# The expert results' gathers of columns 0 to 11: waits on counted tiles, and their sums on GpSimd

## The chip, the cores and the metric

One Trainium2 chip, one of its cores. The metric is the device time of one execution in microseconds (us); a measurement is the median of several executions.

## What is computed

The input x has 2 x 1024 rows of 256 numbers. Each row is layer-normed to xn, and the output is x plus two branches of xn, cut here to what matters:

```python
# attention branch: tokens of 16 numbers, windows of 8, two half-heads with a 3-tap convolution,
# a projection, a layer norm over 16, a residual; written back transposed
# expert branch: 2048 rows, 16 experts, 6 chosen for each row
scores = sigmoid(xn @ gate_weight.T)
topk_idx, topk_weight = gate(scores, bias)      # 2 of 4 groups, then 6 of their 8 experts
for e in range(16):
    inter = silu(xn @ gate_proj[e].T) * (xn @ up_proj[e].T)
    out += comb[:, e:e+1] * (inter @ down_proj[e].T)
out += shared expert of 352 hidden units on every row
return x + attention(xn) + out
```

## The kernel before, in words

The 2048 rows lie in SBUF as 128 lanes by 16 *columns* of 256 numbers; `yacc` holds x in this layout and collects every term of the output. A first stage (to about 104 us) normalises the rows, computes the routing on VectorE (`routing`, L1211) and runs the shared expert. Each chosen pair of row and expert gets a *slot*, a row number in a DRAM table `xs_dram`; `slot_i` holds, for each lane, column c and choice k (0 to 5), the slot at place c * 8 + k, sorted by falling slot. GpSimd scatters the rows to their slots with 96 indirect DMAs (L594), 16 columns by 6 choices.

The experts then run over 111 *tiles* of 128 slots (constant NT; loops over t on all engines, TensorE's at L1055, VectorE's at L1649). Tile t is loaded by SyncE from `xs_dram` (L491), transposed (L981, copied by ScalarE L725), multiplied by the gate and up weights (L991), made to `inter_s` by ScalarE's silu (L733) and VectorE's product (L1532), transposed again (L1007, L740), multiplied by the down weights (L1014), copied to one of four buffers `y_s` (ScalarE L753, in four tiles VectorE L1556) and stored by SyncE to `y_dram` (L496). The semaphore `y_sb` counts these copies, `put[i]` the stores of buffer i that have landed. Three pieces of other work are threaded by hand through the tile loop: the attention of four blocks on VectorE (`attention`, steps per tile by `attention_quota`), whose last step ends about tile 80; transposes and projections on TensorE (tiles 87 to 98); and `normalise` (L1570), one VectorE step per tile from tile 100 on, in which L1598 adds the attention branch to four columns of `yacc` at a time.

Slots are dealt so that early columns come early: an expert's rows are in column order, and the tiles of all experts are dealt in parts that end with columns 5, 9, 12, 14, 15, 16 (`MARKS`). `DONE` gives, for each first column, how many tiles must be stored at most before its results are complete, whatever the routing: 69 for columns 0 to 8, 87 for 9 to 11, 99 for 12 and 13, 105 for 14, 111 for 15.

The results come back by 42 *fetches* (`FETCHES`): seven groups of columns (0-2, 3-5, 6-8, 9-11, 12-13, 14, 15) by six choices. A fetch is one indirect DMA (L614) for each of its columns, into one of seven places (`places`, 768 numbers wide); that makes 72 DMAs for columns 0 to 11 and 24 for the rest. GpSimd issues them in order; before a group it waits for the stores of `DONE` tiles (`stored`, L599), and before a place is filled again it waits that the sum of the fetch before it is done (L607). VectorE adds each fetch to `yacc` (`add_results`, L1605, one instruction at L1614): fetches 0 to 23 at fixed tiles from tile 76 on (`ADD_AT`), the rest among the last steps of `normalise` and behind them. Last, SyncE and ScalarE store the columns (`store_out`, L444).

Of the kernel before, what the change touches and what calls it, by code (L numbers as in the profile page):

```python
# [126 lines left out]
ADD_AT = {}  # L127
for _n in range(24):
    ADD_AT.setdefault(76 + 14 * _n // 9, []).append(_n)


def place_of(n):

    return n % FEW if n < 2 * FEW else n % PLACES
# [61 lines left out]
def build(nc, x, wall, wexp, consts, out):  # L196
    ctx = ExitStack()
    with ctx:
# [16 lines left out]
        y_dram = nc.dram_tensor("y_dram", [NT * P, H], F32).ap()  # L215
# [20 lines left out]
        pad_row = at("pad_row", [1, NE], I32)  # L236
        blk_at = cursor[0]
# [59 lines left out]
        whole = at("whole", [P, (len(MARKS) + 1) * NE], I32)  # L297
        assert cursor[0] <= after_w, cursor[0] - after_w
# [17 lines left out]
        added = sem("added")  # L316
# [140 lines left out]
        def _(sp):  # L457
# [20 lines left out]
            sp.wait_ge(weights_ok, 1)  # L478
            sp.wait_ge(m_ok, UNITS)
# [42 lines left out]
        def _(pool):  # L522
# [80 lines left out]

            for n, (first, last, k) in enumerate(FETCHES):
                if k == 0 and first in DONE:
                    stored(first)
                if before_at(n) is not None:  # L607

                    pool.wait_ge(added, before_at(n) + 1)
                elif n >= FEW:  # L610
                    pool.wait_ge(att_ok, 2 * B)
                for c in range(first, last):
                    o, there = c * KEEP + k, (c - first) * H
                    nc.gpsimd.indirect_dma_start(places[place_of(n)][:, there:there + H], None,  # L614
                                                 y_dram[0:DONE[max(d for d in DONE if d <= first)] * P, :],
                                                 bass.IndirectOffsetOnAxis(slot_i[:, o:o + 1], 0)).then_inc(got[place_of(n)], 16)

# [197 lines left out]
        def _(pe):  # L815
# [41 lines left out]
            def qkv_job(n):  # L857
# [42 lines left out]
            def expert_rows():  # L900
# [3 lines left out]
                                 skip_group_check=True).then_inc(erow_ps, 1)  # L904

# [60 lines left out]
            for s in range(UNITS):  # L966
# [113 lines left out]
        def _(dve):  # L1080
# [130 lines left out]
            def routing():  # L1211
# [154 lines left out]

                one = work[:, 0:1]
# [13 lines left out]
            def tile_experts():  # L1381
# [5 lines left out]
                nc.vector.tensor_scalar(e_row[:, :], misc[0][0:1, 384:384 + RT], float(H), None, ALU.add).then_inc(rows_ok, 1)  # L1387

# [181 lines left out]
            def normalise():  # L1570
# [17 lines left out]
                for b in range(NBLK):  # L1588
# [7 lines left out]
                    settle()  # L1596
                    dve.wait_ge(added, sums.value())
# [21 lines left out]
            for u in range(-1, UNITS):  # L1619
# [29 lines left out]
            for t in range(NT):  # L1649
# [17 lines left out]
                for n in ADD_AT.get(t, ()):  # L1667
                    add_results(n)
# [57 lines left out]
```

## Time and profile before

| | |
|---|---|
| median of 3 runs (lowest to highest) | 457.14 us (451.7 to 457.64) |
| the profiled execution's own time | 456.78 us |
| its span in the profile | 455.0 us |
| TensorE busy | 400.8 us (88%) |
| VectorE busy | 364.8 us (80%) |
| ScalarE busy | 224.8 us (49%) |
| GpSimd busy | 234.7 us (52%) |
| 96 scatters, GpSimd L594 | 111.4 us, 1160 ns each |
| VectorE add of 768 columns, L1614 | 950 ns |

Busy shares are averages over stages. GpSimd's 52% is made of three stretches with long waits between them, and TensorE's 88% ends at 425 us, thirty before the span does. So a stage is read by its own timeline: which engine works without a gap there, and what the others wait for. The start of an instruction is taken from the timeline, and the time that it takes from its queue is the distance to the next start (its spacing), which can be shorter than its duration where the engine overlaps two.

### The profile page before, as it was taken

How to read it: one execution, taken by the hardware profiler on the slowest of the kernel's cores; microseconds unless marked ns; L12 is line 12 of the kernel's file. 1: busy time of each engine (PE TensorE's matmuls, PEld its weight loads, DVE VectorE, ACT ScalarE, POOL GpSimd, SP SyncE). 2: the span in 40 equal slices, each digit the busy share in tenths (PEclk: the TensorE clock that was granted, in tenths of full speed). 3: DMA queues.
4: the chain of work that ended last, by engine and by line, in shares of the span. 5: the costliest groups of instructions: out<-in, count | busy, mean ns of one | idle time of the engine just before them, and what ended most of it. 6: DMA issues, size and time to landing. Idle time of an engine off the chain costs nothing.

```text
span 455.0 us, 7300 instructions
## 1 busy us (share of the span) xinstructions
PE 400.8 (88%) x1989; PEld 310.2 (68%) x1989; DVE 364.8 (80%) x593; ACT 224.8 (49%) x616; POOL 234.7 (52%) x221
## 2 busy tenths in 40 slices
PE   7799599999999999997999999989989999999200
PEld 7688499889767677675777777767667777767200
DVE  2869953686899989999799999999995355479951
ACT  3654234325564445653476864675437744554200
POOL 3530156775777777873000000007787777778671
PEclk9889979999999999999899999999999999999755
DMA  7998422226455766576733334336657997665652
GB/s 169 330 412 354 163 107 88 98 76 223 132 184 190 205 207 197 184 229 184 216 114 103 97 95 121 103 90 169 196 166 202 287 234 194 175 198 160 201 151 81
DMA packets 55878, 80.55 MB, mean 177 GB/s; under 512 B 8480, under 2 KB 47264, under 8 KB 55584
## 3 DMA queue, kind: packets, MB, share of 16 engines
q1 hardware_dynamic: 42912, 50.91, 36.7%
q0 software_dynamic: 9216, 25.96, 18.8%
q10 hardware_dynamic: 3712, 3.21, 2.4%
q8 instruction: 19, 0.31, 0.3%
q14 instruction: 19, 0.16, 0.1%
HBM read 43.48 MB, written 36.57 MB: 176 GB/s over the span
## 4 chain that ended last, share of the span: by engine, by line
PE 49%; DVE 22%; issue 12%; DMA 5%; POOL 4%; ACT 2%; SPq 2%; ACTq 1%; DVEq 1%; POOLq 0%
PE gate L991 15%; PE ps_y L1014 10%; POOL xs_dram L594 4%; PE ps_y L942 4%; DVE prod L1094 4%; DVE qkv L1094 4%; PE up L920 3%; PE ps_y L1007 3%; DVE inter_s L1532 3%; PE up L981 3%; DVE sc L1094 2%; PE gate L920 2%; DVE yacc L1614 2%; PE misc L882 2%; PE misc L1041 2%
## 5 line engine op out<-in xcount | busy, mean ns | idle before, releaser
L991 PE MATMUL gate<-wrec,xgT 128*128 x444 | 151.3, 463 | 2.9 <-ACT xgT L725 1.8
L594 POOL DMA_INDIRECT xs_dram<-xrow,slot_i x96 | 111.4, 1160 | 50.6 <-DMA xs_dram<-xrow,slot_i 21.5
L1014 PE MATMUL ps_y<-wrec,interT 88*128 x444 | 115.2, 382 | 0.0
L614 POOL DMA_INDIRECT gat<-y_dram,slot_i x50 | 55.0, 1099 | 113.6 <-DMA y_dram<-y_s 98.9
L991 PEld LDWEIGHTS gate<-wrec,xgT 128*128 128x128 f32 x444 | 75.8, 190 | 28.2 <-issue 4.4
L1014 PEld LDWEIGHTS ps_y<-wrec,interT 88*128 88x128 f32 x444 | 76.0, 191 | 6.7 <-issue 0.3
L1532 DVE SCALAR_TENSOR_TENSOR inter_s<-gate,xg,gate_s 128x176 f32<-128x176 f32 x111 | 43.6, 393 | 33.8 <-ACT gate_s L733 32.9
L733 ACT ACTIVATE gate_s<-gate 128x176 f32<-128x176 f32 x111 | 35.2, 317 | 70.1 <-PE ps_y L1007 67.7
L753 ACT ACTIVATE y_s<-ps_y 128x256 f32<-128x256 f32 x107 | 41.0, 383 | 55.7 <-PE up L981 52.6
L1007 PEld LDWEIGHTS ps_y<-ident,inter_s 128*88 128x88 f32 x222 | 26.7, 123 | 37.6 <-issue 19.3
L1007 PE MATMUL ps_y<-ident,inter_s 128*88 128x128 f32 x222 | 42.7, 274 | 5.0 <-DVE y_s L1556 2.8
L981 PE MATMUL up<-ident,xg 128*128 128x128 f32 x222 | 42.8, 274 | 3.7 <-DMA xg<-xs_dram 3.7
L981 PEld LDWEIGHTS up<-ident,xg 128*128 128x128 f32 x222 | 31.4, 143 | 15.7 <-DMA xg<-xs_dram 4.5
L725 ACT ACTIVATE xgT<-up 128x256 f32<-128x256 f32 x107 | 40.4, 379 | 0.2 <-PE up L981 0.2
L740 ACT ACTIVATE interT<-ps_y 88x256 f32<-88x256 f32 x107 | 39.9, 373 | 1.1 <-PE ps_y L1007 1.1
L1094 DVE TENSOR_TENSOR prod<-sc,qkv 128x1024 f32<-128x1024 f32 x32 | 38.4, 1215 | 0.1
L1094 DVE TENSOR_TENSOR sc<-sc,prod 128x1024 f32<-128x1024 f32 x28 | 34.1, 1219 | 0.2
L1094 DVE TENSOR_TENSOR prod<-qkv 128x1024 f32<-128x1024 f32 x28 | 33.6, 1216 | 0.0
L1094 DVE TENSOR_TENSOR qkv<-qkv,prod 128x1024 f32<-128x1024 f32 (+1 forms) x28 | 33.0, 1179 | 0.1
L652 ACT ACTIVATE qkv<-misc 128x192 f32<-128x192 f32 x40 | 14.9, 438 | 27.4 <-PE misc L882 18.8
L614 POOL DMA_INDIRECT prod<-y_dram,slot_i x20 | 20.8, 1039 | 6.1 <-issue 5.2
L614 POOL DMA_INDIRECT spare<-y_dram,slot_i x16 | 19.8, 1240 | 5.9 <-issue 3.7
(215 smaller groups left out, 633.8 us busy)
## 6 DMA issues: line engine op xcount, KB each, us to landing
xg<-xs_dram SPq DMA_DIRECT2D x111, 136.0 KB, 2.6
y_dram<-y_s SPq DMA_DIRECT2D x111, 128.0 KB, 2.1
wrec<-wexp SPq DMA_DIRECT2D x14, 608.0 KB, 15.1
xs_dram<-zrow SPq DMA_DIRECT2D x1, 2176.0 KB, 13.0
xn_dram<-xrow SPq DMA_DIRECT2D x8, 256.0 KB
qkv<-xn_dram SPq DMA_DIRECT2D x8, 256.0 KB
xs_dram<-xrow,slot_i POOLq DMA_INDIRECT x96, 2.9
wrec<-wexp SPq DMA_DIRECT2D x1, 1216.0 KB, 5.6
```

The lines of the kernel that those rows point to most:

```text
L594: nc.gpsimd.indirect_dma_start(xs_dram[0:DONE[max(d for d in DONE if d <= c)] * P, :], bass.IndirectOffsetOnAxis(slot_i[:, o:o + 1], 0), x ...
L614: nc.gpsimd.indirect_dma_start(places[place_of(n)][:, there:there + H], None, y_dram[0:DONE[max(d for d in DONE if d <= first)] * P, :], b ...
L725: nc.scalar.activation(xgT[:, t % 2, :], guB[t % 2][:, 0:H], ACT.Copy).then_inc(xt_sb, 1)
L733: nc.scalar.activation(gate_s[:, t % 2, :], guA[t % 2][:, 0:I], ACT.Silu).then_inc(gate_ok, 1)
L740: nc.scalar.activation(interT[:, t % 2, :], ps_y[0:HALF, t % 2 * 2 * H + H:(t % 2 + 1) * 2 * H], ACT.Copy).then_inc(it_sb, 1)
L753: nc.scalar.activation(y_s[:, t % YRING, :], ps_y[:, t % 2 * 2 * H:t % 2 * 2 * H + H], ACT.Copy).then_inc(y_sb, 1)
L981: last = nc.tensor.transpose(guB[t % 2][:, k * P:(k + 1) * P], xg[:, t % RING, k * P:(k + 1) * P], ident[:, :])
L991: last = nc.tensor.matmul(guA[t % 2][:, 0:2 * I], xgT[:, t % 2, k * P:(k + 1) * P], wrec[:, bass.ds(record + k * 2 * I, 2 * I)], start=(k ...
L1007: last = nc.tensor.transpose(ps_y[0:HALF, o:o + P], inter_s[:, t % 2, k * HALF:(k + 1) * HALF], ident[:, :])
L1014: last = nc.tensor.matmul(ps_y[:, t % 2 * 2 * H:t % 2 * 2 * H + H], interT[:, t % 2, k * P:(k + 1) * P], wrec[0:HALF, bass.ds(record + KT ...
L1094: do(nc.vector.tensor_tensor(o, a, b, op))
L1532: nc.vector.scalar_tensor_tensor(inter_s[:, t % 2, :], guA[t % 2][:, I:2 * I], xg[:, t % RING, bass.ds(weight, 1)], gate_s[:, t % 2, :], A ...
```

## The change

For each of the first four groups of three columns (fetches 0 to 23, `OWN`) the kernel now counts the tiles that really have to be done. The highest slot of each lane and column (`tops`) is transposed and reduced to the highest slot of each group, and `tiles_done` turns it into a tile count plus 4 in `done_row`. GpSimd loads these four numbers into registers and waits for `y_sb` to reach them, where it waited for the stores of 69 or 87 tiles: a copy into a `y_s` buffer waits for the store of four tiles before, so the count plus 4 says that the stores have landed. A tiny multiply (L634 of the changed kernel) stands behind the wait.

The sums of fetches 0 to 23 move from VectorE to GpSimd: behind the DMAs of fetch n, it adds fetch n-1 (`own_sum`). These 24 fetches use four places in turn. `ADD_AT` is gone; VectorE keeps fetches 24 to 41. The results are stored into the first 256 numbers of the rows of `xs_dram`, in place of `y_dram`, so GpSimd multiplies `slot_i` by the row's 272 numbers first. In the changed kernel TensorE's second projection job behind the shared expert (L909 there) and SyncE's load of the last two experts' weights (L489 there) also wait for `done_ok`.

```diff
+COUNTED = 4
+OWN = COUNTED * TOP
+TOPS_AT, COUNTS_AT = 8, 10
...
-    return n % FEW if n < 2 * FEW else n % PLACES
+    return n % FEW if n < OWN else n % PLACES
...
-            engine.wait_ge(added, TOP * sum(first < c1 for first, _ in GROUPS))
+            engine.wait_ge(pool_added, min(OWN, TOP * sum(first < c1 for first, _ in GROUPS)))
...
+            sp.wait_ge(done_ok, 1)
             sp.wait_ge(m_ok, UNITS)
...
-                sp.dma_start(y_dram[t * P:(t + 1) * P, :], y_s[:, t % YRING, :]).then_inc(put[t % YRING], 16)
+                sp.dma_start(xs_dram[t * P:(t + 1) * P, 0:H], y_s[:, t % YRING, :]).then_inc(put[t % YRING], 16)
...
+            def own_sum(n):
+
+                first, last, _ = FETCHES[n]
+                acc = yacc[:, first * H:last * H]
+                pool.wait_ge(got[place_of(n)], 16 * fetched(n))
+                if n:
+                    pool.wait_ge(pool_added, n)
+                nc.gpsimd.tensor_tensor(acc, acc, places[place_of(n)][:, 0:(last - first) * H], ALU.add).then_inc(pool_added, 1)
+
+            landed(pool, sent, TOK * TOP)
+            nc.gpsimd.tensor_scalar(slot_i[:, :], slot_i[:, :], float(XW), None, ALU.mult).then_inc(rows_at, 1)
+            pool.wait_ge(rows_at, 1)
+            pool.wait_ge(y_ok, NBLK)
+            pool.wait_ge(done_ok, 1)
+            counted = [nc.gpsimd.value_load(done_row[0:1, g:g + 1], min_val=YRING + 1, max_val=NT) for g in range(COUNTED)]
             for n, (first, last, k) in enumerate(FETCHES):
-                if k == 0 and first in DONE:
+                if k == 0 and n < OWN:
+
+                    pool.wait_ge(y_sb, counted[n // TOP])
+                    nc.gpsimd.tensor_tensor(expo[:, 0:1], expo[:, 1:2], expo[:, 2:3], ALU.mult)
+                elif k == 0 and first in DONE:
                     stored(first)
...
+                if 1 <= n < OWN:
+                    own_sum(n - 1)
+                if n == OWN - 1:
+                    own_sum(n)
...
                 if n == EARLY_JOBS + 1:
 
                     pe.wait_ge(rows_ok, 2)
+                    pe.wait_ge(done_ok, 1)
...
+            def tiles_done():
+
+
+                dve.wait_ge(last_ps, 1)
+                groups = last_f[0:1, 0:COUNTED]
+                do(nc.vector.tensor_reduce(groups, misc[0][0:1, P:P + COUNTED * WIDE].rearrange("p (g c) -> p g c", c=WIDE), AX.X, ALU.max))
+                settle()
+                do(nc.vector.tensor_scalar(last_i[:, :], groups, P - 1.0, None, ALU.add))
+                settle()
+                do(nc.vector.tensor_scalar(last_i[:, :], last_i[:, :], 7, None, ALU.logical_shift_right))
+                settle()
+                nc.vector.tensor_scalar(done_row[:, :], last_i[:, :], float(YRING), None, ALU.add).then_inc(done_ok, 1)
...
+                    dve.wait_ge(pool_added, min(OWN, TOP * sum(first < (b + 1) * TILES for first, _ in GROUPS)))
                     dve.wait_ge(added, sums.value())
...
             y_sum(NBLK - 1)
+            tiles_done()
...
-                for n in ADD_AT.get(t, ()):
-                    add_results(n)
```

The order of GpSimd's instructions at the first fetches, before: the 96 scatters end, and the fetches follow each other with nothing between.

```order
L594 DMA xs_dram<-xrow,slot_i 14208x272 x6
L614 DMA gat<-y_dram,slot_i 128x256 x9
L614 DMA spare<-y_dram,slot_i 128x256 x3
L614 DMA gat<-y_dram,slot_i 128x256 x9
L614 DMA spare<-y_dram,slot_i 128x256 x3
```

The same place on GpSimd in the changed kernel (L605 is the scatter, L647 the fetch's DMA, L622 the sum).

```order
L605 DMA xs_dram<-xrow,slot_i 14208x272 x6
L625 TENSOR_SCALAR slot_i<-slot_i 128x128
...
L634 TENSOR_TENSOR expo<-expo 128x1
L647 DMA gat<-xs_dram,slot_i 128x256 x6
L622 TENSOR_TENSOR yacc<-yacc,gat 128x768
L647 DMA gat<-xs_dram,slot_i 128x256 x3
L622 TENSOR_TENSOR yacc<-yacc,gat 128x768
L647 DMA spare<-xs_dram,slot_i 128x256 x3
L622 TENSOR_TENSOR yacc<-yacc,gat 128x768
```

A sum of 128 x 768 now stands in the one queue behind every three DMAs, 24 in all.

VectorE's order in tiles 75 to 77, before: two steps of attention between the products L1532, and from here on a sum L1614 in most tiles.

```order
L1532 SCALAR_TENSOR_TENSOR inter_s<-gate,xg,gate_s 128x176
L1522 TENSOR_TENSOR qkv<-qkv,prod 128x1024
L1094 TENSOR_TENSOR prod<-sc,qkv 128x1024
L1614 TENSOR_TENSOR yacc<-yacc,gat 128x768
L1532 ISA
L1532 SCALAR_TENSOR_TENSOR inter_s<-gate,xg,gate_s 128x176
L1094 TENSOR_TENSOR prod<-sc,qkv 128x1024
L1094 TENSOR_TENSOR qkv<-qkv,prod 128x1024
L1614 TENSOR_TENSOR yacc<-yacc,gat 128x768
```

The same place on VectorE in the changed kernel (L1606 is the product, L1596 and L1148 are attention).

```order
L1606 SCALAR_TENSOR_TENSOR inter_s<-gate,xg,gate_s 128x176
L1596 TENSOR_TENSOR qkv<-qkv,prod 128x1024
L1148 TENSOR_TENSOR prod<-sc,qkv 128x1024
L1606 ISA
L1606 SCALAR_TENSOR_TENSOR inter_s<-gate,xg,gate_s 128x176
L1148 TENSOR_TENSOR prod<-sc,qkv 128x1024
L1148 TENSOR_TENSOR qkv<-qkv,prod 128x1024
```

The sums are gone from there, and the attention steps stand in the same tiles as before.

VectorE's order at the end of the changed kernel, behind the last product L1606 (L1673 is the add of the attention branch, L1148 its two steps, L1689 `add_results`).

```order
L1606 SCALAR_TENSOR_TENSOR inter_s<-gate,xg,gate_s 128x176
L1148 TENSOR_TENSOR qkv<-qkv,prod 128x256x4
L1148 TENSOR_TENSOR qkv<-qkv 128x256x4
L1673 TENSOR_TENSOR yacc<-yacc,qkv 128x1024
L1689 TENSOR_TENSOR yacc<-yacc,spare 128x512
L1148 TENSOR_TENSOR qkv<-qkv,prod 128x256x4
L1148 TENSOR_TENSOR qkv<-qkv 128x256x4
L1689 TENSOR_TENSOR yacc<-yacc,sc 128x512
L1673 TENSOR_TENSOR yacc<-yacc,qkv 128x1024
L1689 TENSOR_TENSOR yacc<-yacc,prod 128x512 x2
```

The first sum that VectorE does is that of fetch 24 (into the place `spare`), behind the third L1673.

## Rows read from the trace of the kernel before

**Rows 1.** The page: the span, and GpSimd's busy tenths in 40 slices.
```profile
span 455.0 us, 7300 instructions
POOL 3530156775777777873000000007787777778671
```

**Rows 2.** L614: what GpSimd sat idle for before it (us, times), and time to landing.
```profile
  DMA y_dram<-y_s: 98.9, 2
DMA to landing us min/median/max: 2.7/3.4/6.4
```

**Rows 3.** Timeline of GpSimd: start us, us, engine, line, operation; fetches' DMAs 1, 25, 73, 91, 96.
```profile
308.58 1.93 POOL L614 DMA_INDIRECT gat<-y_dram,slot_i  x1 [97.89 <-DMA y_dram<-y_s]
...
345.30 1.41 POOL L614 DMA_INDIRECT gat<-y_dram,slot_i  x1 [0.30 <-issue]
...
409.29 1.04 POOL L614 DMA_INDIRECT spare<-y_dram,slot_i  x1 [0.30 <-issue]
...
437.81 1.08 POOL L614 DMA_INDIRECT gat<-y_dram,slot_i  x1 [0.30 <-issue]
...
445.45 0.95 POOL L614 DMA_INDIRECT prod<-y_dram,slot_i  x1 [0.30 <-DVE yacc L1614]
```

**Rows 4.** Timeline of ScalarE and VectorE: two copies into y_s.
```profile
281.80 0.38 ACT L753 ACTIVATE y_s<-ps_y 128x256 f32<-128x256 f32 x1 [0.50 <-PE up L981]
...
306.14 0.41 DVE L1556 COPY y_s<-ps_y 128x256 f32<-128x256 f32 x1
```

**Rows 5.** Stretches: us; busy (count) of PE, PEld, DVE, ACT, POOL; PEclk, DMA share, GB/s.
```profile
282.00:345.00 63.00, 59.56 (x282) 43.09 (x281) 61.04 (x79) 35.47 (x102) 29.40 (x24) 1.00 0.51 147
345.00:409.00 64.00, 62.94 (x326) 46.74 (x325) 35.08 (x65) 37.05 (x108) 49.37 (x48) 1.00 0.80 217
```

**Rows 6.** Timeline of GpSimd: arithmetic on two inputs in SBUF, and a cast.
```profile
19.43 1.82 POOL L548 TENSOR_TENSOR w_lo<-raw,w_hi 128x768 fp32r<-128x768 f32 x1
21.20 0.89 POOL L554 CAST w_hi<-raw 128x768 fp32r<-128x768 f32 x1
...
44.52 1.29 POOL L559 TENSOR_TENSOR in_lo<-sil,in_hi 128x512 fp32r<-128x512 f32 x1 [17.77 <-ACT in_hi L674]
```

**Rows 7.** Timeline of VectorE in the same stretches.
```profile
18.65 0.40 DVE L1122 TENSOR_SCALAR xrow<-yacc,rstd,mv 128x256 f32<-128x256 f32 x1
...
19.57 1.83 DVE L1122 TENSOR_SCALAR xrow<-yacc,rstd,mv 128x256 f32<-128x256 f32 x1
21.33 0.68 DVE L1113 TENSOR_TENSOR xT_lo<-misc,xT_hi 128x512 fp32r<-128x512 f32 x1
...
45.04 0.90 DVE L1094 TENSOR_TENSOR sc<-sc 128x112 f32<-128x112 f32 x1
...
46.40 0.87 DVE L1094 TENSOR_TENSOR sc<-sc 128x112 f32<-128x112 f32 x3
```

**Rows 8.** Timeline of VectorE: the last attention step, and a sum.
```profile
338.40 1.23 DVE L1524 TENSOR_TENSOR qkv<-qkv,prod 128x1024 f32<-128x1024 f32 x1
339.54 0.95 DVE L1614 TENSOR_TENSOR yacc<-yacc,gat 128x768 f32<-128x768 f32 x1
340.41 0.40 DVE L1532 SCALAR_TENSOR_TENSOR inter_s<-gate,xg,gate_s 128x176 f32<-128x176 f32 x1
```

**Rows 9.** Timeline of VectorE at the end.
```profile
420.48 0.40 DVE L1532 SCALAR_TENSOR_TENSOR inter_s<-gate,xg,gate_s 128x176 f32<-128x176 f32 x1
...
430.34 1.88 DVE L1598 TENSOR_TENSOR yacc<-yacc,qkv 128x1024 f32<-128x1024 f32 x1
...
448.25 0.43 DVE L1614 TENSOR_TENSOR yacc<-yacc,prod 128x256 f32<-128x256 f32 x1 [0.46 <-DMA prod<-y_dram,slot_i]
```

**Rows 10.** Timeline of VectorE and TensorE behind the shared expert.
```profile
104.35 1.66 DVE L1407 SCALAR_TENSOR_TENSOR yacc<-ps_y,cst,yacc 128x256 f32<-128x256 f32 x4 [0.66 <-PE ps_y L942]
...
106.07 0.55 PE L882 MATMUL ps_y<-blk_hi,xT_hi 128*128 128x384 f32 x1 [0.35 <-DVE yacc L1407]
```

**Rows 11.** The chain that ended last, before tile 39 starts: start us, us, what.
```profile
209.55 2.63 DMA xs_dram<-xrow,slot_i
```

More of the change, by code:

```diff
@@ L236, in build @@
         pad_row = at("pad_row", [1, NE], I32)
+        done_row = at("done_row", [1, COUNTED], I32)
         blk_at = cursor[0]
@@ L297, in build @@
         whole = at("whole", [P, (len(MARKS) + 1) * NE], I32)
+        tops = at("tops", [P, TOK])
+        top = at("top", [TOK, 1])
+        last_f = at("last_f", [1, TOK])
+        last_i = at("last_i", [1, COUNTED], I32)
         assert cursor[0] <= after_w, cursor[0] - after_w
@@ L315, in build @@
         got = [sem(f"got{i}") for i in range(PLACES)]
-        added = sem("added")
+        added, pool_added = sem("added"), sem("pool_added")
+        rows_at = sem("rows_at")
+        tops_ok, tops_ps, top_ok, last_ps, done_ok = sem("tops_ok"), sem("tops_ps"), sem("top_ok"), sem("last_ps"), sem("done_ok")
         masks, zeros, gen, stat = sem("masks"), sem("zeros"), sem("gen"), sem("stat")
@@ L447, in store_out @@
             engine.wait_ge(norm_ok, (c1 - 1) // TILES + 1)
-            engine.wait_ge(added, TOP * sum(first < c1 for first, _ in GROUPS))
+            engine.wait_ge(pool_added, min(OWN, TOP * sum(first < c1 for first, _ in GROUPS)))
+            if TOP * sum(first < c1 for first, _ in GROUPS) > OWN:
+                engine.wait_ge(added, TOP * sum(first < c1 for first, _ in GROUPS) - OWN)
             for run, b_of, r in lane_runs():
@@ L614, in _ @@
                     nc.gpsimd.indirect_dma_start(places[place_of(n)][:, there:there + H], None,
-                                                 y_dram[0:DONE[max(d for d in DONE if d <= first)] * P, :],
+                                                 xs_dram[0:DONE[max(d for d in DONE if d <= first)] * P, :].rearrange("r (w o) -> (r w) o", o=1),
                                                  bass.IndirectOffsetOnAxis(slot_i[:, o:o + 1], 0)).then_inc(got[place_of(n)], 16)
+                if 1 <= n < OWN:
+                    own_sum(n - 1)
+                if n == OWN - 1:
+                    own_sum(n)
         @block.scalar
@@ L904, in expert_rows, with column_tops, tops_in_row @@
                                  skip_group_check=True).then_inc(erow_ps, 1)
+            def column_tops():
+                pe.wait_ge(tops_ok, 1)
+                pe.wait_ge(rows_ok, 2)
+                nc.tensor.transpose(misc[0][0:TOK, 0:P], tops[:, :], ident[:, :]).then_inc(tops_ps, 1)
+            def tops_in_row():
+                pe.wait_ge(top_ok, 1)
+                nc.tensor.matmul(misc[0][0:1, P:P + TOK], top[:, :], ident[0:TOK, 0:TOK], start=True, stop=True,
+                                 skip_group_check=True).then_inc(last_ps, 1)
             def gate_up(u, between):
@@ L973, in _ @@
                     expert_rows()
+                if s == TOPS_AT:
+                    column_tops()
+                if s == COUNTS_AT:
+                    tops_in_row()
             def columns(t):
@@ L1632, in _ @@
                     tile_experts()
+                if u == TOPS_AT + 2:
+                    column_max()
                 for _ in range(HEADS_PLAN.get(u, 0)):
@@ L1673, in _ @@
                 if i % 2:
-                    add_results(sums.value())
-            for n in range(sums.value(), len(FETCHES)):
+                    add_results(OWN + sums.value())
+            for n in range(OWN + sums.value(), len(FETCHES)):
                 add_results(n)
```

15 lines of the change are left out of this document (9 added, 6 removed).

## The prediction

> **What bounds the kernel now.** I read first the page's slices, to see who works at the end. GpSimd shows nothing from slice 20 to 26 and then runs at 7 or 8 tenths to the end of the span [rows 1]. What it waited for in the gap is a store of results: 98.9 us in two waits [rows 2]. Then the timeline: its first fetch starts at 308.58, its 96th and last at 445.45 [rows 3], and between them it issues one DMA after another; the 0.30 us of "issue" between two is there each time. The last product of the tile loop starts at 420.48 and TensorE is done some 5 us behind it, so the last 30 us belong to GpSimd's queue; behind its last DMA come a landing, an add on VectorE at 448.25 [rows 9] and the store of a column. The spacing of the DMAs differs by stage [rows 3]: 24 from 308.58 to 345.30, 1.53 us each; 48 to 409.29, 1.33 us each; the last six from 437.81 to 445.45, 1.27 us each. The first of these stages is the one in which VectorE is full with attention: 61.04 of 63 us, against 35.08 of 64 behind it [rows 5]. From the last fetch's start to the end of the span it is 455.0 - 445.45 = 9.55 us, and the profiled execution took 456.78, that is 1.78 more than its span. So the kernel's time is now: start of the first fetch, plus the length of GpSimd's queue, plus 11.3 us.
>
> **The counted wait: how much earlier the fetches start.** Routing the reference's inputs by hand through the dealing of slots gives 56, 57, 62 and 81 tiles for the four groups, so GpSimd waits for 60, 61, 66 and 85 copies. The copy at 306.14 is that of tile 68, the last of the 69 of before, and its store landed when the first fetch started at 308.58. Tile 59, the 60th, was copied at 281.80 + 0.38 = 282.2 [rows 4]. The head start is 308.6 - 282.2 = 26.4 us. The groups of 61 and 66 wait for nothing, since six fetches before them take longer; the fourth needs tile 84, 16 tiles behind the copy at 306.14 and so copied before 365 even in a slowed loop, far ahead of its turn (below).
>
> **The sums: what they put into GpSimd's queue.** 24 additions of 128 x 768 with both inputs in SBUF. The same shape stands in the trace as L548: 1.82 us, and 21.20 - 19.43 = 1.77 to the next instruction [rows 6]. Behind it I put the 0.3 us that stands between any two DMAs of this queue: 2.1 us beside an idle VectorE. In the full stage GpSimd may also find VectorE at an instruction of 1.1 us spacing [rows 8]; I take half of that, 0.5, so 2.6. The fetched numbers are no cause of waiting: a DMA lands in 3.4 us (median) [rows 2], and three others are issued before its sum. Only the last sum has none before it but sum 22: 3.4 - 1.8 = 1.6 us of waiting. The four tiny multiplies I take at 0.3 each, 1.2 together; the multiply of `slot_i`, the register loads and the other waits lie in the queue's idle time before 282.
>
> **The sums: what they do to VectorE.** L1122 takes 0.40 us at 18.65 and 1.83 us at 19.57, ending when GpSimd's L548 ends; L1094 on 112 numbers takes 0.90 us beside L559, and 0.29 each (0.87 for three) behind it. L1113, one of whose inputs is in PSUM, keeps 0.68 at 21.33, behind that L548 [rows 6, 7]. So a GpSimd addition holds a VectorE instruction with SBUF inputs to its end. Nearly all attention steps have two. I take 1.6 us of VectorE per addition in the full stage, where the sum it did itself cost 340.41 - 339.54 = 0.87 [rows 8]. Attention ends at 339.6 now; its remaining work at 282.2 is 57.4 less four sums of 0.87, 53.9 us. With a loss of 1.6 in every turn of 7.2 us (3 x 1.53 + 2.6) it takes 53.9 / (1 - 0.22) = 69.3 us and ends at 351.5, 12 us later than now. The tile loop goes with it, and TensorE ends at about 437, 12 us later than now. That costs nothing, since GpSimd is later still.
>
> The Trainium skill, "SBUF — State Buffer", "Who interferes with whom", says this as a rule: VectorE and GpSimd share one pair of SBUF ports, and a VectorE instruction with two SBUF inputs and a GpSimd instruction that reads SBUF exclude each other for a whole instruction. By that rule nearly every sum in the full stage stalls VectorE and GpSimd in turn, as I have priced it; the trace shows the stall for the two pairs above. Without the rule the sum below would be about 5 us less (no 0.5 per sum, and the slower spacing ends at 336).
>
> **The rest.** `tiles_done` puts four tiny VectorE instructions (0.8 us together by the 0.2 of one such) behind the last L1407, which ends at 106.02, and TensorE's second projection job, run now before L1407 is done, waits for them: its third, now at 106.07 [rows 10], starts about 1.5 us later. The tile loop starts that much later, but it waits later for GpSimd's last scatter (at 209.55) [rows 11], which does not depend on it but for a loose pacing; so I count 0, with 1.5 at most. The stores into rows of 272 numbers and the fetches from there move the same 1 KB each: 0. VectorE's relief behind tile 80 (24 sums) lies beside the longer queue of GpSimd: 0.
>
> **The sum.** 282.2, and then in GpSimd's queue:
> - to 351.5, 69.3 us: 9.6 turns of 7.2, that is 29 DMAs and 9.6 sums;
> - the other 43 DMAs of the own fetches at 1.33 and 14.4 sums at 2.1: 57.2 + 30.2 = 87.4, to 438.9; with 1.6 and 1.2 from above 441.7;
> - the 24 DMAs of fetches 24 to 41, 23 spacings of 1.27: 29.2, so the last starts at 470.9. VectorE's sums of one or two columns (0.43 to 0.7) keep up with them, and all tiles are stored by then.
> - 9.55 to the end of the span: 480.5; 1.78 more: **482 us**.
>
> Against the profiled 456.78 that is +25; the median of the runs shown, 457.14, is the same within 0.4. The ratio is 1.055.
>
> **The bounds.** Below: every sum costs its bare 1.77 and no stage is stretched: 282.2 + 29 x 1.53 + 43 x 1.33 + 29.2 + 24 x 1.77 + 11.3 = 467. Above: every sum waits for a whole attention step and has a slow turn from adding to issuing DMAs, 3.3 us each: 282.2 + 44.4 + 57.2 + 29.2 + 79.2 + 2.8 + 11.3 = 506. The trace shows no such turn with its cost, which is why the upper end is loose; I take the nearer rows, and a range of 467 to 498.
>
> **The rivals.**
> 1. *The head start wins.* If a sum costs GpSimd less than 26.4 / 24 = 1.1 us, the queue ends earlier than before. It would have to lie in the time that the queue loses now. For it: "issue" gaps of 0.3 and stretched DMAs. Against it: L548 has a spacing of 1.77, and those gaps stand between DMAs, not behind a sum. Then the end is set by the places: Fetch 31 goes into `spare`, which VectorE frees only behind the third L1673. Tile 110's work on VectorE, begun with the product at 420.48 now [rows 9], comes some 3 us earlier without the sums of tiles 76 to 82; three steps of 1.2, 1.9 for the add L1598 [rows 9] and 0.7 for the sum put that place free at about 424, and with the steps and adds of the last block between its sums VectorE frees the third such place at about 430; eight more spacings bring the last DMA to 440 to 443: span 450 to 452, 453 us. Not slower.
> 2. *The counts do not help, the sums cost.* If the counted wait ends near the old one (a count that takes in later tiles), the start is 308, and the sums add 24 x 2.3: 26 us more than forecast, 508 us. Against it: the counts follow from the inputs.
> 3. *The port decides.* If GpSimd's sum and VectorE's steps go by turns and each waits the other out in full (1.2 more per sum on GpSimd over most of the tile loop, which is itself stretched by 1.8 per sum), GpSimd's queue grows by another 24 x 0.6 to 24 x 1: 495 to 506, say 500 us. For it: rows 7. Against it: VectorE is little over half full behind tile 82.
>
> **How the numbers follow.** A measurement of this kernel tells about 2% from no change. Forecast 0.76; rival 1 0.08, of which half ends below -2%; rival 3 0.10, rival 2 0.02; the rest, 0.04, is a queue whose sums are just absorbed, with a time near that of before. Only the first and the last are not slower by over 2%: faster 0.04, same 0.08, slower 0.88.
>
> **What would show it.** GpSimd's first fetch at about 282, its 72nd at about 435 (it is at 408 now, one spacing ahead of 409.29) and its last at about 471. The sums near 1.8 us with attention steps beside them of up to 3 us in place of 1.2; attention ends near 351 and TensorE near 437. In the chain of waits GpSimd's lines fill the last hundred us. The forecast is wrong if a sum's turn costs GpSimd under 1.1 us, or if the first fetch does not start near 282, or if the last fetches wait for VectorE.

## The result, and the profile after

The changed kernel takes **469.15 us** (median; 467.39 to 472.82), the kernel before on the same chip 454.42 (450.66 to 457.64). The ratio is 1.036, with a 95% interval of 1.024 to 1.049: slower, by 14.7 us. Some executions of a kernel come out over 1.5% longer than its fastest; they are in the medians given here and left out of the ratios. The prediction said slower, 482 us (467 to 498). The profiled execution of the changed kernel, 472.82 us, is the slowest of its four; its span is 471.0.

The page: the span, GpSimd's slices, and the chain that ended last.

```profile
span 471.0 us, 7331 instructions
...
POOL 2612176864787777770000008888888888888872
...
PE 38%; POOL 33%; issue 10%; DVE 8%; DMA 5%; SPq 2%; ACT 1%; ACTq 1%; POOLq 0%; DVEq 0%
```

The gap of zeros ends with slice 24, where it ended with slice 27 in [rows 1], and then stands an 8 in every slice to the 38th. GpSimd is 33% of the chain, from the first fetch on. Before, the chain went through TensorE's tile loop and VectorE's last steps, and GpSimd was 4% of it:

```profile
PE 49%; DVE 22%; issue 12%; DMA 5%; POOL 4%; ACT 2%; SPq 2%; ACTq 1%; DVEq 1%; POOLq 0%
```

So the bound is now GpSimd's queue, as forecast for the last hundred us; it holds from 282 on.

GpSimd's timeline at the first fetches: start us, us, engine, line, operation.

```profile
281.48 0.49 POOL L634 TENSOR_TENSOR expo<-expo 128x1 f32<-128x1 f32 x1 [68.89 <-ACT y_s L790]
282.13 1.84 POOL L647 DMA_INDIRECT gat<-xs_dram,slot_i  x1 [0.16 <-issue]
...
303.77 1.82 POOL L622 TENSOR_TENSOR yacc<-yacc,gat 128x768 f32<-128x768 f32 x1
305.75 1.77 POOL L647 DMA_INDIRECT gat<-xs_dram,slot_i  x1 [0.17 <-POOL yacc L622]
307.83 1.12 POOL L647 DMA_INDIRECT gat<-xs_dram,slot_i  x1 [0.30 <-issue]
309.26 0.95 POOL L647 DMA_INDIRECT gat<-xs_dram,slot_i  x1 [0.30 <-issue]
```

VectorE in the same stretch, and its last attention step.

```profile
301.88 1.91 DVE L1550 TENSOR_REDUCE mx<-sc 128x128 f32<-128x1024 f32 x1
303.82 2.86 DVE L1553 TENSOR_TENSOR sc<-sc,mx 128x1024 f32<-128x1024 f32 x1
...
346.35 1.22 DVE L1598 TENSOR_TENSOR qkv<-qkv,prod 128x1024 f32<-128x1024 f32 x1
```

The step at 303.82 is one of 1.2 us. It starts 0.05 us behind the sum at 303.77 and ends at 306.68, that is one step's length behind the end of the sum at 305.6: it was held by the sum. The DMA that GpSimd starts at 305.75 lies beside it and takes 1.77 us in place of 0.95.

GpSimd behind the attention, where VectorE is half idle.

```profile
361.63 0.97 POOL L647 DMA_INDIRECT gat<-xs_dram,slot_i  x1 [0.16 <-POOL yacc L622]
...
364.17 0.96 POOL L647 DMA_INDIRECT gat<-xs_dram,slot_i  x1 [0.30 <-issue]
365.14 1.83 POOL L622 TENSOR_TENSOR yacc<-yacc,gat 128x768 f32<-128x768 f32 x1
367.14 0.97 POOL L647 DMA_INDIRECT gat<-xs_dram,slot_i  x1 [0.16 <-POOL yacc L622]
```

A *turn* is what one fetch puts into the queue, three DMAs and one sum: here 367.14 - 361.63 = 5.51 us. The sum begins 0.01 us behind the third DMA, and the next DMA 0.16 behind the sum: it fills the place of one 0.30 us gap.

The end of GpSimd's queue (DMAs 72, 73 and 96, the last two own sums).

```profile
421.42 1.14 POOL L647 DMA_INDIRECT spare<-xs_dram,slot_i  x1 [0.30 <-issue]
422.57 1.82 POOL L622 TENSOR_TENSOR yacc<-yacc,gat 128x768 f32<-128x768 f32 x1
424.54 2.62 POOL L622 TENSOR_TENSOR yacc<-yacc,spare 128x768 f32<-128x768 f32 x1
427.95 1.82 POOL L647 DMA_INDIRECT spare<-xs_dram,slot_i  x1 [0.80 <-POOL yacc L622]
...
461.48 0.96 POOL L647 DMA_INDIRECT prod<-xs_dram,slot_i  x1 [0.30 <-DVE yacc L1689]
```

The stretches of the changed kernel: full stage, quiet stage, end (us; busy and count of PE, PEld, DVE, ACT, POOL; PEclk, DMA share, GB/s), to be read against [rows 5].

```profile
282.00:357.00 75.00, 67.61 (x304) 48.36 (x303) 70.93 (x77) 38.42 (x111) 65.36 (x50) 0.95 0.55 154
357.00:428.00 71.00, 69.73 (x354) 51.37 (x352) 37.22 (x53) 39.62 (x116) 60.72 (x51) 1.00 0.66 177
428.00:462.00 34.00, 3.38 (x16) 2.39 (x16) 17.68 (x23) 2.13 (x6) 26.99 (x24) 0.62 0.57 159
```

From 282 to 462 GpSimd is busy for 153 of 180 us, and the rest is gaps of up to 0.31 us, but for one of 0.80 before the 73rd DMA. GpSimd's queue from its first to its 96th DMA is 461.48 - 282.13 = 179.35 us; it was 445.45 - 308.58 = 136.87 [rows 3]. So the start is 26.4 us earlier, the queue 42.5 longer, and the end 16.0 later.

### The profile page after: what moved, and what is told of

It reads as the page before. It is cut to its first block, busy times and chain, and to the rows that moved or that the text cites. A ratio compares the mean times of both kernels' runs of the same rounds, so it can differ in the third digit from the quotient of the medians.

```text
span 471.0 us, 7331 instructions
## 1 busy us (share of the span) xinstructions
PE 404.2 (86%) x1992; PEld 311.7 (66%) x1992; DVE 365.5 (78%) x575; ACT 224.2 (48%) x616; POOL 284.8 (60%) x250
## 4 chain that ended last, share of the span: by engine, by line
PE 38%; POOL 33%; issue 10%; DVE 8%; DMA 5%; SPq 2%; ACT 1%; ACTq 1%; POOLq 0%; DVEq 0%
POOL gat L647 14%; POOL yacc L622 10%; PE gate L1045 9%; PE ps_y L1068 7%; POOL spare L647 5%; PE up L970 4%; PE ps_y L992 3%; PE gate L970 3%; PE misc L920 3%; DVE sc L1148 3%; POOL xs_dram L605 2%; PE ps_y L1061 2%; PE up L1035 2%; PE ps_y L920 2%; POOL prod L647 2%
## 5 line engine op out<-in xcount | busy, mean ns | idle before, releaser
L1045 PE MATMUL gate<-wrec,xgT 128*128 x444 | 153.9, 470 | 7.9 <-DVE inter_s L1606 7.5
L605 POOL DMA_INDIRECT xs_dram<-xrow,slot_i x96 | 114.1, 1188 | 50.0 <-DMA xs_dram<-xrow,slot_i 20.2
L1606 DVE SCALAR_TENSOR_TENSOR inter_s<-gate,xg,gate_s 128x176 f32<-128x176 f32 x111 | 43.4, 392 | 44.0 <-ACT gate_s L770 43.9
L647 POOL DMA_INDIRECT gat<-xs_dram,slot_i x62 | 67.0, 1080 | 16.4 <-issue 14.3
L1148 DVE TENSOR_TENSOR prod<-sc,qkv 128x1024 f32<-128x1024 f32 x32 | 44.6, 1410 | 0.1
L634 POOL TENSOR_TENSOR expo<-expo 128x1 f32<-128x1 f32 x4 | 1.1, 286 | 68.9 <-ACT y_s L790 68.9
L1148 DVE TENSOR_TENSOR prod<-qkv 128x1024 f32<-128x1024 f32 x28 | 36.2, 1310 | 0.0
L1148 DVE TENSOR_TENSOR qkv<-qkv,prod 128x1024 f32<-128x1024 f32 (+1 forms) x28 | 34.6, 1236 | 0.1
L1148 DVE TENSOR_TENSOR sc<-sc,prod 128x1024 f32<-128x1024 f32 x28 | 34.1, 1217 | 0.2
L622 POOL TENSOR_TENSOR yacc<-yacc,gat 128x768 f32<-128x768 f32 x18 | 33.6, 1869 | 0.3
L647 POOL DMA_INDIRECT spare<-xs_dram,slot_i x22 | 25.7, 1166 | 6.3 <-issue 4.6
```

What stands on the lines that cost most here:

```text
L605: nc.gpsimd.indirect_dma_start(xs_dram[0:DONE[max(d for d in DONE if d <= c)] * P, :], bass.IndirectOffsetOnAxis(slot_i[:, o:o + 1], 0), x ...
L622: nc.gpsimd.tensor_tensor(acc, acc, places[place_of(n)][:, 0:(last - first) * H], ALU.add).then_inc(pool_added, 1)
L1045: last = nc.tensor.matmul(guA[t % 2][:, 0:2 * I], xgT[:, t % 2, k * P:(k + 1) * P], wrec[:, bass.ds(record + k * 2 * I, 2 * I)], start=(k ...
L1148: do(nc.vector.tensor_tensor(o, a, b, op))
L1606: nc.vector.scalar_tensor_tensor(inter_s[:, t % 2, :], guA[t % 2][:, I:2 * I], xg[:, t % RING, bass.ds(weight, 1)], gate_s[:, t % 2, :], A ...
```

## The experiments

Eight kernels; on the same chips the kernel before had medians of 453.6 to 454.7 us. Profiles of kernels that are alike up to the first fetch (all but experiment 2) put it between 275.9 and 284.3, so mechanisms are compared by lengths within the queue, not by absolute times. "Full turn" is the mean spacing of the fetches 1 to 11 (ten turns), "quiet turn" one behind the attention. "Tiles 66 to 90" is the time from VectorE's product of tile 66 to that of tile 90. All of them keep the stores into `xs_dram`. The diffs are against the changed kernel unless said otherwise, and only their main lines are shown.

**1. The counts without the sums.** GpSimd waits for the counts, and VectorE makes all sums, one in 1.7 tiles from tile 66 on.

```diff
-OWN = COUNTED * TOP
+OWN, EARLY = 0, COUNTED * TOP
+ADD_AT = {}
+for _n in range(24):
+    ADD_AT.setdefault(66 + 17 * _n // 10, []).append(_n)
...
-    return n % FEW if n < OWN else n % PLACES
+    return n % FEW if n < EARLY else n % PLACES
...
-                if k == 0 and n < OWN:
+                if k == 0 and n < EARLY:
...
+                for n in ADD_AT.get(t, ()):
+                    add_results(n)
```

> The changed kernel's counted waits and stores, but all sums on VectorE again (fetches 0 to 23 at tiles 66 to 105, one in 1.7 tiles). Theory A (GpSimd's queue sets the end, and its 24 sums made the change slow): the first fetch starts at about 282, the queue is 24 sums (43 us) shorter than in the changed kernel, so it runs ahead of the tiles and the last six fetches start when tile 110 is stored, near 432; the last fetch starts near 440, the time is 445 to 452 us, below both kernels. Rival B (the counted waits, the register loads or the stores into rows of 272 cost the time): it stays near the changed kernel's 469. Rival C (VectorE's order at the end sets the time, whoever fetches early): within 1% of before, 450 to 458.

Measured: 459.73 us, ratio 1.011 (0.998 to 1.023): none of the three expected times, nearest to rival C's 450 to 458. First DMA at 280.75, last at 447.61. GpSimd's 73rd DMA and VectorE's sum that it waited for:

```profile
412.34 1.16 POOL L649 DMA_INDIRECT spare<-xs_dram,slot_i  x1 [16.05 <-DVE yacc L1690]
```
```profile
410.59 0.95 DVE L1690 TENSOR_TENSOR yacc<-yacc,spare 128x768 f32<-128x768 f32 x1
```

The queue stood for 16 us. Its place was freed only by sum 23, which the table puts at tile 105. Waits of 4.5 us for such places stand before it at 384.8 and 392.8. A head start of 28 us is worth nothing where VectorE's order hands the places back at the old time.

**2. The sums without the counts.**

```diff
-                if k == 0 and n < OWN:
-
-                    pool.wait_ge(y_sb, counted[n // TOP])
-                    nc.gpsimd.tensor_tensor(expo[:, 0:1], expo[:, 1:2], expo[:, 2:3], ALU.mult)
-                elif k == 0 and first in DONE:
+                if k == 0 and first in DONE:
```

> The changed kernel, but GpSimd waits for 69 and 87 stored tiles as before; the sums stay on GpSimd. Theory A: the first fetch starts near 308, the queue keeps nearly its length of 179 us (a little less, since fewer sums meet a full VectorE), so the last fetch starts near 485 and the time is 490 to 497 us. If the counted wait bought nothing (rival: something else sets the changed kernel's end), it stays near 469.

Measured: 489.54 us, ratio 1.081 (1.072 to 1.090), just under the expected 490 to 497 and 20.4 us above the changed kernel; first DMA at 303.73, last at 478.12. So with the old waits GpSimd's sums cost 35 us, and the counts give 20 of them back. In the profiled executions the first DMA is 21.6 us later than in the changed kernel and the last 16.6: the queue is 5.0 us shorter (174.4), since fewer of its sums lie beside the attention. Most of the head start reaches the end, because the queue never waits.

**3. Neither sum.** The 24 sums become one-number products: columns 0 to 11 miss their expert results.

```diff
-                nc.gpsimd.tensor_tensor(acc, acc, places[place_of(n)][:, 0:(last - first) * H], ALU.add).then_inc(pool_added, 1)
+                there = places[place_of(n)]
+                nc.gpsimd.tensor_tensor(there[:, 0:1], there[:, 1:2], there[:, 2:3], ALU.mult).then_inc(pool_added, 1)
```

> Each of GpSimd's 24 sums of 768 numbers is replaced by a product of one number per lane in its place, so the fetches of columns 0 to 11 are not added at all. Theory A: the queue loses 24 x 1.65 = 40 us, so it is bound by the tiles: time 440 to 450 us. It also shows rival 1 of the prediction in its pure form (sums that cost GpSimd nothing), worked out there as 453. If it stays above 460, the sums' length was not what made the change slow.

Measured: 446.04 us, ratio 0.984 (0.973 to 0.995). GpSimd's 73rd and last DMA:

```profile
395.23 0.98 POOL L648 DMA_INDIRECT spare<-xs_dram,slot_i  x1 [8.27 <-issue]
...
419.24 1.69 POOL L648 DMA_INDIRECT spare<-xs_dram,slot_i  x1 [5.08 <-DVE yacc L1690]
...
435.98 0.95 POOL L648 DMA_INDIRECT prod<-xs_dram,slot_i  x1 [0.30 <-DVE yacc L1690]
```

The rival in which the head start wins needs cheap sums, and with sums that cost next to nothing it holds, even 7 us better than its 453. The 8.27 us before the 73rd DMA are the wait for the stores of 99 tiles: the 99th copy into `y_s` ends at 392.63. The 5.08 us at 419.24, before the DMA of fetch 31, are the wait for a place that VectorE frees, which is that rival's chain. Where the queue waits like this, an emptier queue gains nothing.

Full turn 48.7 / 10 = 4.87 us, against the changed kernel's (350.42 - 286.89) / 10 = 6.35. The 1.48 between them is a sum less the tiny product in its place, and that product takes 0.2 to 0.7 us here. The 30 DMAs of the ten turns have the same mean duration in both kernels, 1.21 us. So a sum lengthens no DMA on average; it costs its own length, 1.92 us over these ten, less 0.13 for the gap that it fills: 1.8 us in the full stage.

**4. Writing without reading.** Each sum becomes two memsets of the place; columns 0 to 11 again miss their results.

```diff
-                nc.gpsimd.tensor_tensor(acc, acc, places[place_of(n)][:, 0:(last - first) * H], ALU.add).then_inc(pool_added, 1)
+                nc.gpsimd.memset(places[place_of(n)], 0.0).then_inc(rows_at, 1)
+                pool.wait_ge(rows_at, n + 2)
+                nc.gpsimd.memset(places[place_of(n)], 0.0).then_inc(pool_added, 1)
```

> Each of GpSimd's 24 sums is replaced by two clears of the same place, which read nothing from SBUF and together take about 1.7 us; the fetches of columns 0 to 11 are not added. If sums hold up VectorE by a port that only a reading GpSimd instruction takes, no attention step is above 1.3 us, attention ends some 8 to 10 us earlier than in the changed kernel, and TensorE with it; and if GpSimd's queue alone sets the end, the time still stays within 2% of the changed kernel's 469. If the tile loop's delay were the cause of the loss, the time would fall to about 459. If any GpSimd instruction holds up VectorE, the attention steps stay stretched to 2.5.

Measured: 460.69 us, ratio 1.016 (1.003 to 1.029); first DMA at 275.87, last at 447.15. GpSimd, then VectorE, in the full stage:

```profile
301.67 0.76 POOL L622 MEMSET spare<- 128x768 f32 x1
302.49 0.74 POOL L624 MEMSET spare<- 128x768 f32 x1
303.38 1.20 POOL L649 DMA_INDIRECT gat<-xs_dram,slot_i  x1 [0.16 <-POOL spare L624]
```
```profile
301.40 1.21 DVE L1150 TENSOR_TENSOR prod<-qkv,cst 128x1024 f32<-128x1024 f32 x1
302.64 1.09 DVE L1150 TENSOR_TENSOR qkv<-qkv,prod 128x896 f32<-128x896 f32 x1
```

The attention steps beside the memsets keep their 1.1 to 1.2 us. Tiles 66 to 90 take 62.0 us, against 73.1 in the changed kernel and 65.2 before, where VectorE has its own sums. The time alone doesn't decide: 460.69 lies between "within 2% of 469" and "about 459". The traces do. GpSimd's queue waits only once, 2.31 us for the landing of its own last fetch, and never for a tile. It is 179.35 - 171.28 = 8.1 us shorter than the changed kernel's, since two memsets take 1.5 us and a sum 1.9, and the median is 8.5 us lower. (In the profiled executions the last DMA is 14.3 us earlier, 6.3 of them by an earlier first fetch.) The last attention step ends at 329.1, in the changed kernel at 347.6. So the time follows the queue, and the 11 us of tile loop are worth nothing.

**5. Reading one input.** Each sum becomes two copies of the place onto itself (results missing as above).

```diff
-                nc.gpsimd.tensor_tensor(acc, acc, places[place_of(n)][:, 0:(last - first) * H], ALU.add).then_inc(pool_added, 1)
+                nc.gpsimd.tensor_copy(places[place_of(n)], places[place_of(n)]).then_inc(rows_at, 1)
+                pool.wait_ge(rows_at, n + 2)
+                nc.gpsimd.tensor_copy(places[place_of(n)], places[place_of(n)]).then_inc(pool_added, 1)
```

> Each of GpSimd's 24 sums is replaced by two copies of the place onto itself: they read and write SBUF, one input each, 0.89 us each by the cast of the kernel before; the fetches of columns 0 to 11 are not added. In the run with clears no VectorE step was held up. If a GpSimd instruction that reads SBUF takes VectorE's second input whatever its own number of inputs, the attention steps stretch by about 0.9 us here (to some 2.1), and the tile loop is longer from tile 66 to 90 than in the run with clears (62 us), towards the 76 us of the changed kernel. If only two-input instructions do, it stays at 62. Either way GpSimd's queue sets the end: 171 us as with clears, plus 24 x (1.9 - 1.5), about 180; time within 2% of 469.

Measured: 478.69 us in the profiled execution, whose span is 476.9; the only other one took 535.37, with a granted clock of 0.74 against 0.93, so there is no ratio. Queue 467.41 - 282.98 = 184.4 us. GpSimd, then VectorE:

```profile
306.83 0.83 POOL L622 COPY gat<-gat 128x768 f32<-128x768 f32 x1
307.73 1.72 POOL L624 COPY gat<-gat 128x768 f32<-128x768 f32 x1
```
```profile
306.23 2.52 DVE L1150 TENSOR_TENSOR qkv<-qkv,cst 128x1024 f32<-128x1024 f32 x1
308.79 1.73 DVE L1150 TENSOR_TENSOR prod<-qkv,cst 128x1024 f32<-128x1024 f32 x1
```

One input is enough: VectorE is held (2.52 us for 1.2), and the second copy waits for VectorE in turn (1.72 for 0.83). Tiles 66 to 90 take 72.3 us, nearly the changed kernel's 73.1 (the 76 of the expectation goes one tile too far). The Trainium skill, "SBUF — State Buffer", "Who interferes with whom", says that a VectorE instruction with two SBUF inputs contends with a GpSimd instruction that reads SBUF and not with one that only writes it; experiments 4 and 5 agree, 62.0 against 72.3 us for the same tiles.

**6. VectorE's order mended.** From experiment 1, with the diff against it: sums 10 to 23 at tiles 82 to 98, 24 to 29 at tiles 105 to 110, and places turned so that fetches from 24 on start with the free ones.

```diff
-for _n in range(24):
-    ADD_AT.setdefault(66 + 17 * _n // 10, []).append(_n)
+for _n in range(30):
+    ADD_AT.setdefault(66 + 17 * _n // 10 if _n < 10 else 82 + 5 * (_n - 10) // 4 if _n < 24 else 81 + _n, []).append(_n)
...
-    return n % FEW if n < EARLY else n % PLACES
+    return n % FEW if n < EARLY else (n - 20) % PLACES
```

> From e1 (counted waits, sums on VectorE). In e1 the 73rd DMA waited 16 us for the place that sum 23 held until tile 105, and the places of fetches 31 to 36 for VectorE's last steps. Here sums 10 to 23 stand at tiles 82 to 98, where VectorE has idle time, fetch 24 takes the place `sc`, which is free, and sums 24 to 29 stand at tiles 105 to 110. If the order of the sums on VectorE is what took the head start in e1, the last DMA starts when the last tile is stored and five spacings on, near 438, and the time is 446 to 450 us, 1 to 2% below before and well below e1's 459.7. If it stays at 455 or above, something else is late (the steps of normalise themselves, or the longer tile loop).

Measured: 455.3 us (12 executions), ratio 1.007 (1.002 to 1.012); the expected 446 to 450 was missed. The profiled execution took 459.8. One of VectorE's sums, then GpSimd's 73rd DMA:

```profile
387.39 0.96 DVE L1690 TENSOR_TENSOR yacc<-yacc,gat 128x768 f32<-128x768 f32 x1 [1.29 <-DMA gat<-xs_dram,slot_i]
```
```profile
410.82 0.96 POOL L649 DMA_INDIRECT sc<-xs_dram,slot_i  x1 [17.85 <-DMA xs_dram<-y_s]
```

The wait for the place is gone, and another has taken it, that for tile 99. VectorE now stands in the tile loop for the landing of fetched numbers, 1.3 us here and up to 4.3 at other tiles, with the next product behind it; tiles 66 to 90 take 76.1 us (69.6 in experiment 1), and the last tile's product starts at 431.06 and not at 422.51. The head start was spent on a slower tile loop.

**7. Each sum twice.** (Columns 0 to 11 get their expert results twice.)

```diff
+                nc.gpsimd.tensor_tensor(acc, acc, places[place_of(n)][:, 0:(last - first) * H], ALU.add).then_inc(rows_at, 1)
+                pool.wait_ge(rows_at, n + 2)
```

> The changed kernel with each of GpSimd's 24 sums done twice. If the queue sets the end, the last fetch moves by 24 x 1.9 = 46 us and the time is 469 + 46 = 512 to 518 us, whatever the tile loop does (it gets longer by the port, and still ends far ahead). If part of a sum lay beside other work of the queue, it would be less than 40.

Measured: 525.0 us, ratio 1.165 (1.152 to 1.177), above the expected 512 to 518. Queue 511.35 - 280.20 = 231.15 us, 51.8 more than in the changed kernel: 2.16 for each of 24 further sums, where 1.9 was expected. The quiet turn grows from 5.50 to 7.38, by 1.88, the full turn from 6.35 to 8.93, by 2.58 (the last of these ten turns lie behind the attention; the first seven mean 9.4). The difference stands in the second sum; GpSimd, then VectorE:

```profile
298.17 1.83 POOL L622 TENSOR_TENSOR yacc<-yacc,gat 128x768 f32<-128x768 f32 x1
300.08 2.67 POOL L624 TENSOR_TENSOR yacc<-yacc,gat 128x768 f32<-128x768 f32 x1
```
```profile
297.56 3.54 DVE L1150 TENSOR_TENSOR prod<-qkv 128x1024 f32<-128x1024 f32 x1
301.13 2.71 DVE L1150 TENSOR_TENSOR sc<-sc,prod 128x1024 f32<-128x1024 f32 x1
```

Held by the first sum, the VectorE step runs between the two, and the second sum pays for it: 0.84 us more. It is so in six of the seven pairs beside the attention.

**8. Half each.** VectorE adds fetches 0 to 11, in the full stage and just behind it, and GpSimd adds fetches 12 to 23; places from fetch 24 on as in experiment 6.

```diff
-OWN = COUNTED * TOP
+OWN, HALVES = COUNTED * TOP, 2 * TOP
...
+for _n in range(HALVES):
+    ADD_AT.setdefault(66 + 17 * _n // 10, []).append(_n)
+for _n in range(24, 28):
+    ADD_AT.setdefault(83 + _n, []).append(_n)
...
-                if 1 <= n < OWN:
+                if HALVES + 1 <= n < OWN:
```

> Counted waits as in the changed kernel; VectorE adds fetches 0 to 11 (tiles 66 to 84, 0.87 us each, in the stage in which a GpSimd sum costs most on both engines) and GpSimd adds fetches 12 to 23, where VectorE is half idle. Fetches 24 to 27 are added at tiles 107 to 110, and the places of fetches from 24 on turn so that the places free earliest come first. Theory A (a sum costs GpSimd about 2 us beside attention and 1.7 us behind it, nothing else): first DMA about 281, 12 spacings of fetches of 4.6 us to 336, then 36 DMAs of 1.27 and 12 sums of 1.7 to about 402, so the 73rd DMA starts near 402 and the last near 432 to 440, span 442 to 450, time 444 to 452: a gain of 1 to 3% over the kernel before. Theory B (what VectorE frees at the end sets the last fetches, as in the runs without GpSimd sums): 73rd DMA near 402 but the last fetches wait for places or sums and the last starts at 445 or later, time 455 to 460, no gain. The sums beside the attention steps should be gone, so no attention step over 2 us before 350.

Measured: 452.02 us (448.19 to 455.69, 12 executions), ratio 0.997 (0.993 to 1.001). GpSimd's first DMA, its first and last sum, its 73rd and its last DMA:

```profile
278.63 1.84 POOL L654 DMA_INDIRECT gat<-xs_dram,slot_i  x1 [0.16 <-issue]
...
345.48 1.83 POOL L628 TENSOR_TENSOR yacc<-yacc,gat 128x768 f32<-128x768 f32 x1
...
404.47 1.81 POOL L628 TENSOR_TENSOR yacc<-yacc,spare 128x768 f32<-128x768 f32 x1 [2.06 <-DMA spare<-xs_dram,slot_i]
406.42 1.93 POOL L654 DMA_INDIRECT sc<-xs_dram,slot_i  x1
...
441.31 0.96 POOL L654 DMA_INDIRECT gat<-xs_dram,slot_i  x1 [0.30 <-issue]
```

Theory A is met in mechanism and time, at the late edge: the 73rd DMA 4 us later than expected, the last 1 us behind its bound; its gain of at least 1% is not reached. The first stage is 3.6 us longer than expected, a fetch taking (332.37 - 283.39) / 10 = 4.90 us and not 4.6, and the stage behind it 2.9, of which 2.06 are the wait for the landing of the last own fetch; an earlier first DMA (278.63 for 281) gives 2.4 back. With half the sums the queue is 162.7 us, 16.7 shorter than the changed kernel's. It has the lowest median of those that compute everything, and cannot be told from the kernel before.

## Why the prediction was right, point by point

**What bounded the kernel before**, read loosely. The prediction gave the last 30 us to GpSimd's queue. The queue was the last in line there, but it stood twice:

```profile
428.01 1.18 POOL L614 DMA_INDIRECT gat<-y_dram,slot_i  x1 [1.04 <-DMA y_dram<-y_s]
430.50 2.54 POOL L614 DMA_INDIRECT spare<-y_dram,slot_i  x1 [1.31 <-DVE yacc L1614]
```

The first wait is for the store of the last tile, the second for a place that VectorE frees. So a shorter queue alone would have gained next to nothing, while a longer one costs almost at once. For a change that lengthens it, the sum could be built on the queue.

**The start**, right. 282.13 for 282.2. The later groups waited for nothing. That it agrees to 0.1 us is luck: the 60th copy ended 0.8 us earlier than in the kernel before (281.39), the tiny multiply and two gaps took 0.7, and other profiles of the same start have it up to 6 us earlier and 2 us later.

**The full stage**, right in mechanism, the turn too large. 33 DMAs and 10 sums took 350.42 - 282.13 = 68.3 us; by the forecast's terms they would have taken 75.5: minus 7.2. A turn was 6.35 us and not 7.2, a sum 1.8 (experiment 3) and not 2.6. Two pieces of the 2.6 were wrong. The 0.3 us behind a sum isn't there: a sum takes the place of a gap. And the 0.5 for meeting VectorE was put on top of DMA spacings that already hold such meetings: 1.53 us is a spacing stretched by the attention [rows 3], and a sum moves that stretch into the one DMA behind it (1.77 at 305.75) while the other two come off with less, with the same mean of 1.21 us as without sums. The sums themselves are hardly longer: the 24 take 45.5 us, 1.90 each.

**The quiet stage**, mis-sized. 12 turns took 417.20 - 350.42 = 66.8 us, forecast 73.1: minus 6.3. The sum is 1.69 and not 2.1 (minus 4.9), and the DMAs came at 1.27 and not 1.33 (36 of them, minus 2.2); two tiny multiplies and a last turn of 5.9 took a little back. The 1.33 had a cause that the change removes, VectorE's own sums. Before, VectorE's and then GpSimd's timeline:

```profile
369.42 0.95 DVE L1614 TENSOR_TENSOR yacc<-yacc,sc 128x768 f32<-128x768 f32 x1
...
373.42 0.95 DVE L1614 TENSOR_TENSOR yacc<-yacc,prod 128x768 f32<-128x768 f32 x1
```
```profile
369.96 1.22 POOL L614 DMA_INDIRECT gat<-y_dram,slot_i  x1 [0.31 <-issue]
371.49 0.95 POOL L614 DMA_INDIRECT gat<-y_dram,slot_i  x1 [0.30 <-issue]
...
373.99 1.20 POOL L614 DMA_INDIRECT gat<-y_dram,slot_i  x1 [0.30 <-issue]
```

The DMAs that meet a sum of VectorE take 1.2 us, those between them 0.95. Of the ten over 1.1 us from 345.30 to 407.23, nine lie beside such a sum. The forecast carried this over as a property of the queue.

**The last own fetch and sums**: 10.75 us (417.20 to 427.95), where the forecast had 8.2 for the instructions and 1.6 of waiting; the tiny multiplies, 1.2 on their own there, lie in the turns above. Together these three put the 73rd DMA at 427.95 and not 441.7: -7.2 - 6.3 + 0.95 - 1.2 = -13.8.

**The last 24 DMAs**, too short, in the other direction. 461.48 - 427.95 = 33.5 us, forecast 29.2. They lie beside VectorE's steps of `normalise`, and the spacing of 1.27 had been read from the six behind those (437.81 in [rows 3] is the 90th DMA, not the 91st). [rows 3] held the warning: these 23 spacings took 445.45 - 409.29 = 36.2 us before, the waits of 1.04 and 1.31 among them. One of them, VectorE and then GpSimd:

```profile
437.86 1.88 DVE L1673 TENSOR_TENSOR yacc<-yacc,qkv 128x1024 f32<-128x1024 f32 x1
```
```profile
437.94 2.64 POOL L647 DMA_INDIRECT prod<-xs_dram,slot_i  x1 [0.30 <-issue]
```

So the last DMA is 9.4 us earlier than forecast, and tail (9.5) and surroundings (1.8) are as forecast: 472.8 for 482 in the profiled execution. The median lies another 3.7 below it.

**The size**, right by some luck. The forecast was 25 us slower, measured are 14.7. The terms of the lower bound put the 73rd DMA at 282.2 + 44.4 + 57.2 + 42.5 = 426.2, and it came at 427.95, where the forecast had 441.7: up to there the bound was the better forecast. The last 24 DMAs then took 4.3 us more than either had. Without this error in the other direction the median would have been about 465, below the range.

**VectorE and TensorE**, right, a little too large. The last attention step ended at 347.6, 8.0 later than [rows 8], forecast 12; the product of the last tile started at 428.84, 8.4 later than [rows 9]. Nine sums ran until then. Eight of them held a step, 12.2 us longer together than the same steps before; the ninth, at 316.90, fell on two steps with one input (a TENSOR_REDUCE and a RECIPROCAL), which kept their length. That is 1.4 us for each sum and not 1.6. That this costs no time was forecast, and experiment 4 shows it.

**The rivals.** The head start wins: its chain through the places exists (the 5.08 us of experiment 3), but only the kernel without sums gets there. The counts don't help: excluded by 282.13 and by experiment 2, which is that rival made real (489.5, forecast for it 508; its sums were over-priced like the forecast's). The port decides: it needed longer sums in the quiet stage, and they are 1.82 there. A fourth, that the stores into `xs_dram` cost the time, was not tested apart; with them experiment 3 is faster than the kernel before and experiment 8 as fast, so they can't be what makes the 14.7 us.

## What to carry to other kernels

When work moves from a half idle engine to the end of another's queue, price it by what it adds to that queue, and add a transfer's head start to the same sum: here 24 x 1.7 to 1.8 us and some waiting against 26 us. A mean spacing read from the kernel before already contains the collisions that the change removes or moves; separate the bare spacing (1.27 us) from the stretched one before adding a new cost on top. An earlier start is only worth what the next fixed order lets through: a place freed at tile 105 or the store of tile 99 took it back twice.

## What was not expected of the hardware

An indirect DMA on GpSimd is stretched beside VectorE instructions with two inputs in SBUF: 0.95 us alone, 1.20 to 1.22 beside a 0.95 us sum, 1.77 behind its own sum in the full stage, up to 2.64 beside a 1.88 us add. The traces say how. Over all ten profiles 193 of the fetches' DMAs take over 1.2 us, and 175 of them end 0.79 to 0.87 us behind the end of a VectorE instruction with two inputs: the one above at 437.94 ends at 440.58, and VectorE's add beside it at 439.74. It looks as if such a DMA stood until that instruction ends. The 29 DMAs that lay beside a TENSOR_REDUCE or RECIPROCAL, with one input, from their start on took 0.94 to 0.99 us. This is read from starts and ends; no experiment takes it apart.

Two additions of GpSimd in a row behave otherwise than one: the first takes 1.83 us and holds VectorE, the second 2.67 (experiment 7). A GpSimd memset of 768 columns (0.75 us) leaves VectorE's steps as they are, a copy of the same size (0.83) does not.
